# Convolution and attention in two layers: turn and sums in the score banks, the reciprocals in eight pieces, and the weighing two tiles behind

## The reference, cut to what matters

```python
# x: (8, 512, 32, 32), so B = 8 images, C = 512 channels, N = 1024 positions; 8 heads of D = 64
# layer 0: linear attention without softmax, batch norm over (image, position)
K, Q, V = conv1x1(X, Wq, bq), conv1x1(X, Wk, bk), conv1x1(X, Wv, bv)   # (b, 8, 64, 1024)
M = einsum('bhmn,bhen->bhme', K, V)
Out = conv1x1(einsum('bhme,bhmn->bhen', M, Q), Wo, bo) + X
Out = (Out - mean) * rsqrt(var + 1e-5) * gamma + beta
# layer 1: group norm, softmax attention, projection, residual
xn = group_norm(Out, 32 groups)
q, k, v = split(w_qkv @ xn + b_qkv)                                    # 8 heads each
weight = softmax((q / 64**.25)^T (k / 64**.25))                        # 1024 x 1024 per head
hid = v weight^T
return Out + w_proj @ hid + b_proj
```

## Time and profile before

| | before |
|---|---|
| median of 3 runs | 2682.73 us (2681.97 to 2682.75) |
| the profiled execution | 2683.36 us, its span 2681.8 us |
| TensorE matmul busy | 2582.5 us, 96% of the span |
| VectorE, ScalarE, GpSimd busy | 1621.5, 964.6, 1164.3 us |
| DMA over the span | 79 GB/s |

### The profile page before, as it was taken

How to read it: one execution, slowest core, us unless ns; L and a number is a source line. 1 busy time by engine, 2 the same in 40 slices (tenths; PEclk the granted TensorE clock), 3 DMA queues, 4 the chain that set the end, 5 groups by cost and what they waited for, 6 DMA issues and landing times.

```text
span 2681.8 us, 38121 instructions
## 1 busy us (share of the span) xinstructions
PE 2582.5 (96%) x13876; PEld 1710.9 (64%) x13876; DVE 1621.5 (60%) x1756; ACT 964.6 (36%) x1154; POOL 1164.3 (43%) x590
## 2 busy tenths in 40 slices
PE   7999999997999999999999999999999999999998
PEld 6888888886655665565557555755665565557554
DVE  6555455545576737755764667467647746664665
ACT  3333223332343433433442443343433433432433
POOL 4230000000276546564573676375654645761762
PEclk9999999999999999999999999999999999999999
DMA  5330111113202230231205111401231141103001
GB/s 185 130 132 33 47 47 63 63 63 111 110 24 79 87 126 24 95 128 70 102 17 181 40 79 61 152 24 80 102 110 41 78 175 38 79 18 109 17 16 63
DMA packets 64195, 214.34 MB, mean 80 GB/s; under 512 B 9152, under 2 KB 9152, under 8 KB 63168
## 3 DMA queue, kind: packets, MB, share of 16 engines
q1 hardware_dynamic: 49504, 159.41, 16.5%
q0 software_dynamic: 14560, 52.96, 5.4%
HBM read 141.05 MB, written 71.30 MB: 79 GB/s over the span
## 4 chain that ended last, share of the span: by engine, by line
PE 72%; DVE 15%; issue 6%; POOL 4%; ACT 2%; DVEq 0%; ACTq 0%; POOLq 0%
PE psum L1135 16%; PE psum L1380 14%; PE psum L1363 11%; PE psum L1320 7%; PE psum L1154 6%; PE psum L1330 5%; DVE a_all L999 4%; POOL a_all L528 4%; PE psum L1178 4%; PE psum L1206 3%; DVE small L964 3%; DVE r_all L955 2%; DVE r_all L1032 2%; ACT r_all L632 1%; PE psum L1252 1%
## 5 line engine op out<-in xcount | busy, mean ns | idle before, releaser
L528 POOL TENSOR_TENSOR a_all<-a_all 128x1024 f32<-128x1024 f32 x410 | 989.9, 2414 | 715.5 <-ACT a_all L701 680.6
L964 DVE TENSOR_REDUCE small<-psum 128x2 f32<-128x1024 f32 x481 | 589.3, 1225 | 377.8 <-PE psum L1330 377.6
L701 ACT ACTIVATE a_all<-psum 128x1024 f32<-128x1024 f32 x512 | 496.4, 1021 | 496.7 <-PE psum L1363 491.7
L1363 PE MATMUL psum<-r_all 64*128 64x512 f32 x4096 | 517.6, 391 | 1.5 <-ACT a_all L701 1.4
L1380 PE MATMUL psum<-a_all 128*64 128x512 f32 x2048 | 495.7, 605 | 1.4 <-DVE a_all L999 1.4
L1135 PE MATMUL psum<-r_all 128*128 128x512 f32 x1920 | 452.3, 393 | 7.0 <-DVE r_all L1032 5.8
L1363 PEld LDWEIGHTS psum<-r_all 64*128 64x128 f32 x4096 | 385.2, 185 | 88.9 <-ACT a_all L701 11.0
L1135 PEld LDWEIGHTS psum<-r_all 128*128 128x128 f32 x1920 | 357.6, 188 | 101.8 <-DVE r_all L837 11.6
L1320 PE MATMUL psum<-r_all 128*128 128x512 f32 x1536 | 377.2, 402 | 30.6 <-issue 11.8
L1320 PEld LDWEIGHTS psum<-r_all 128*128 128x128 f32 x1536 | 290.5, 192 | 133.6 <-DVE r_all L955 32.7
L1380 PEld LDWEIGHTS psum<-a_all 128*64 128x64 f32 x2048 | 124.3, 136 | 230.4 <-issue 174.0
(11 more groups left out here) (130 smaller groups left out, 1866.0 us busy)
## 6 DMA issues: line engine op xcount, KB each, us to landing
r_all<-w_dram SPq DMA_DIRECT2D x48, 1024.0 KB, 4.9
xn_dram<-a_all POOLq DMA_DIRECT2D x56, 512.0 KB, 3.8
r_all<-xn_dram SPq DMA_DIRECT2D x7, 4096.0 KB, 15.3
a_all<-y_dram SPq DMA_DIRECT2D x9, 2048.0 KB, 7.8
a_all<-x SPq DMA_DIRECT2D x16, 1024.0 KB, 6.6
y_dram<-a_all SPq DMA_DIRECT2D x16, 1024.0 KB, 4.2
out<-a_all SPq DMA_DIRECT2D x32, 512.0 KB, 3.2
w_dram<-r_all POOLq DMA_DIRECT2D x16, 512.0 KB, 3.6
```

The lines of the kernel that those rows point to most:

```text
L528: pool.tensor_tensor(p_sum[:, :, cols], probs[:, 0, :, cols] if i == 1 else p_sum[:, :, cols], probs[:, i % SLOTS, :, cols], ALU.add).then ...
L701: act.activation(probs[:, i % SLOTS, :, cols], psum[half][:, :, :], ACT.Exp, scale=SCALE).then_inc(probs_ready, 1)
L964: dve.reduce_max(max2[:, :, tile, half], psum[3][:, :, :], AX_X).then_inc(work_free, 2)
L1363: last = pe.matmul(psum[half][:, h], k[rows_], q[rows_], start=(t == 0), stop=(t == 3))
```

## The change

1. **Turn and sums move.** The turn goes to `psum[0]`, the sums to `psum[1]`, the two score banks, which are idle between two pairs. ScalarE copies the sums to SBUF (`copy_sums`), and the score halves of the first key tile wait until the turn is read and the sums are copied. The second q/k tile no longer stands behind the turn in `psum[3]`. For p = 0 the turn now comes ahead of the first q/k tile.
2. **Reciprocals.** They read the copy in SBUF, in place, in eight pieces of 128 columns: two after each of the first three q/k parts, the last two behind max tiles 1 and 3.
3. **The fourth q/k tile** goes to a bank of `psum[2]`, and the first max tile is an ordinary one in `psum[3]`.
4. **VectorE's other parts move back**: `normalise` behind max tiles 5 and 7 (before: ahead of and behind the first max tile), `hid_lo` behind 9 and 11 (before: 1 and 2). ScalarE's `hid_hi` moves behind the exponentials of key tiles 3 and 4.
5. **The weighing lags two tiles** (`LAG = 2`): S0 M S1 M S2 M W0 M S3 M W1 ... S7 M W5 M W6 M W7.
6. **Loops**: TensorE, VectorE and ScalarE's loops over the images of layer 1 get `hint_back_edge=True`, a branch hint at the head.
7. **M in layer 0** multiplies 128 columns in place of 256: the same 52 matmuls per image.

In the diff `copy_sums` stands in ScalarE's block, `invert_sums` and the loop over the max tiles in VectorE's, the rest in TensorE's. The two small copies for the next image's norm (line 1093), which stood behind max tile 4 of the pair p = 1, stand before the first max tile of p = 0 now.

```diff
-            def qk_tile(slot, i, before=lambda j: None):
-                piece, cols, to = i // 2, slice(i % 2 * HALF, (i % 2 + 1) * HALF), next_tile()
+            def qk_tile(slot, i, before=lambda j: None, fourth=False):
+                piece, cols = i // 2, slice(i % 2 * HALF, (i % 2 + 1) * HALF)
+                to = psum[2][:, 0] if fourth else next_tile()
...
-                pe.transpose(next_tile()[:, 0:P], max_cols.rearrange("p h t -> p (h t)"), eye).then_inc(work_full, 1)
-                return work.upto()
+                pe.transpose(psum[0][:, 0, 0:P], max_cols.rearrange("p h t -> p (h t)"), eye).then_inc(turn_full, 1)
...
+            def copy_sums(pairs):
+
+                act.wait_ge(o_normed, ONE + pairs * NH)
+                act.wait_ge(sums_full, ONE + pairs + 1)
+                act.activation(recip, psum[1][:, :, :], ACT.Copy).then_inc(sums_copied, 1)
...
+            def invert_sums(pairs, first, n):
+
+                if first == 0:
+                    dve.wait_ge(sums_copied, ONE + pairs + 1)
+                for piece in range(first, first + n):
+                    part = recip[:, piece // CT, piece % CT * P:(piece % CT + 1) * P]
+                    dve.reciprocal(part, part).then_inc(sums_inverted, 1)
...
-                        for m in range(1, MAXES):
+                        for m in range(MAXES):
                             max_tile(m)
-                            if p and m <= NH:
-                                hid_lo(b, p - 1, m - 1)
+                            if m == 0:
+                                next_qk(QK - 1)
+                            if p:
+                                if m in (1, 3):
+                                    invert_sums(pairs - 1, 6 + m // 2, 1)
+                                if m in (5, 7):
+                                    normalise(pairs - 1, m // 7)
+                                if m in (9, 11):
+                                    hid_lo(b, p - 1, m // 11)
...
                     for i in range(NT):
                         scores(pairs, par, i)
                         next_max()
-                        if i:
-                            weigh(b, p, i - 1, more)
+                        if i >= LAG:
+                            weigh(b, p, i - LAG, more)
                             next_max()
-                    weigh(b, p, NT - 1, more)
+                    for i in range(NT - LAG, NT):
+                        weigh(b, p, i, more)
+                        if i < NT - 1:
+                            next_max()
...
-            with pe.Fori(0, B - 1) as b:
+            with nc.Fori(0, B - 1, engines=[pe.engine], hint_back_edge=True) as b:
...
-                            pe.matmul(bank(g)[:, 0:2 * P], ts[:, t, o, g * P:(g + 1) * P], w_q[:, w, o, window],
+                            pe.matmul(bank(g)[:, 0:P], ts[:, t, o, part], w_q[:, w, o, part],
```

More of the change, by code:

```diff
@@ L625, in norm_row, with qk_hi @@
                 act.activation(hi_slot[:, j % 2], raw[j], ACT.Copy).then_inc(xn_hi_done, 1)
-            def qk_hi(pair, par, i):
-                n, ps = work.next()
-                act.wait_ge(work_full, n)
+            def qk_hi(pair, par, i, fourth=None):
+                if fourth is not None:
+                    ps = psum[2][:, 0]
+                    act.wait_ge(fourth_full, fourth)
+                else:
+                    n, ps = work.next()
+                    act.wait_ge(work_full, n)
                 of_k, cols = i // 2, slice(i % 2 * HALF, (i % 2 + 1) * HALF)
@@ L665, in batch1 @@
                     for i in range(QK):
[L666 to L667 removed]
                         if more:
[L669 to L671 removed]
+                            qk_hi((p + 1) % PAIRS, par, i, pairs + 1 if i == QK - 1 else None)
+                        if p and i == 0:
+                            copy_sums(pairs - 1)
                     for i in range(NT):
@@ L707, in batch1 @@
                     if more:
-                        for _ in range(MAXES - 1):
+                        for _ in range(MAXES):
                             work.next_pair()
@@ L723, in batch1 @@
                     norm_rows(range(1))
+                if not last:
+                    copy_sums(b * PAIRS + PAIRS - 1)
                 for h in range(NH):
@@ L947, in _, with qk_lo @@
             work = Tally()
-            def qk_lo(pair, par, i, count):
-                n, ps = work.next()
+            def qk_lo(pair, par, i, count, fourth=False):
+                ps = psum[2][:, 0] if fourth else work.next()[1]
                 of_k, cols = i // 2, slice(i % 2 * HALF, (i % 2 + 1) * HALF)
@@ L1097, in batch1 @@
                     else:
-                        normalise(pairs - 1, 1)
+                        invert_sums(pairs - 1, 0, PIECES)
+                        for h in range(NH):
+                            normalise(pairs - 1, h)
                         for i in range(1, NT):
@@ L1105, in batch1 @@
                     for h in range(NH):
[L1106 removed]
+                        invert_last(pairs, h)
                         normalise(pairs, h)
@@ L1111, in batch1 @@
                         v_tile(b + 1, i)
-                        if i in (1, 2):
-                            invert_sums(pairs, i - 1)
-                        if i in (3, 4):
-                            normalise(pairs, i - 3)
-                        if i in (5, 6):
-                            hid_lo(b, PAIRS - 1, i - 5)
+                        if 1 <= i <= 4:
+                            invert_sums(pairs, 2 * (i - 1), 2)
+                        if i == 5:
+                            for h in range(NH):
+                                normalise(pairs, h)
+                        if i in (6, 7):
+                            hid_lo(b, PAIRS - 1, i - 6)
                 for t, (o, half) in enumerate(proj_tiles(last)):
@@ L1332, in max_tile @@
                 last.then_inc(work_full, 2)
-            def max_first(par, pairs):
-                pe.wait_ge(sums_read, ONE + pairs * NH)
-                for h in range(2):
-                    rows_ = slice(h * D, (h + 1) * D)
-                    last = pe.matmul(psum[2][:, h], q_hl[rows_, par, HI, 0:P], k_hl[rows_, par, HI, 0:HALF], start=True, stop=True)
-                last.then_inc(max0_full, 1)
             def max_turn(pairs):
                 pe.wait_ge(max_ready, pairs + 1)
-                pe.transpose(next_tile()[:, 0:P], max_cols.rearrange("p h t -> p (h t)"), eye).then_inc(work_full, 1)
-                return work.upto()
+                pe.transpose(psum[0][:, 0, 0:P], max_cols.rearrange("p h t -> p (h t)"), eye).then_inc(turn_full, 1)
             def v_tile(i):
@@ L1356, in scores @@
                     pe.wait_ge(probs_ready, ONE + pairs * 2 * NT + (2 * (i - 1) + half + 1 if i else 0))
+                    if i == 0 and half == 0:
+                        pe.wait_ge(turn_read, pairs + 1)
+                    if i == 0 and half == 1:
+                        pe.wait_ge(sums_copied, ONE + pairs)
                     for t, (k, q) in enumerate(((k_hl[:, par, HI, keys], q_hl[:, par, HI, cols]),
@@ L1393, in sums @@
                     for h in range(2):
-                        last = pe.matmul(psum[2][h * D:(h + 1) * D, half], ones64, p_sum[:, h, half * HALF:(half + 1) * HALF],
+                        last = pe.matmul(psum[1][h * D:(h + 1) * D, half], ones64, p_sum[:, h, half * HALF:(half + 1) * HALF],
                                          start=True, stop=True)
                 last.then_inc(sums_full, 1)
+            LAG = 2
             pe.sem_inc(pv_done, ONE)
```

125 lines of the change are left out of this document (58 added, 67 removed).

## The result

| | before | after |
|---|---|---|
| median | 2682.74 us (2681.97 to 2684.0, 4 runs) | 2698.24 us (2696.07 to 2699.26, 4 runs) |
| the profiled execution | 2683.36 us, span 2681.8 | 2696.07 us, span 2694.6 |

The ratio is 1.0055 (95% interval 1.0042 to 1.0069): slower by 15.5 us, where +23.5 was forecast. As in the prediction, an insert is one of the four instructions (two `normalise`, two `hid_lo`) that VectorE does between max tiles, and a hold is the time by which GpSimd's next add comes later because of one.

The account below looks back on a forecast made before the run. TensorE's own list bounds the kernel, busy 49.1 of a pair's 50.16 us. Terms -11.5 - 20 + 62 - 3 - 4 = +23.5; 2683.4 + 23.5 - 0.6 = 2706 us, 8-in-10 range 2646 to 2757.

Parts of the forecast that it names:

- The inserts (+62): VectorE's `normalise` and `hid_lo` among max tiles wait for GpSimd's adds, locking rounds at 5.5 us: +62 us with first steps.
- The signs named for it: In pairs p > 0: rounds of 5.4 to 5.6 us, max tiles waiting 0.9 to 1.1, inserts of 2.3 to 2.6.
- Rival A: Inserts among max tiles stay as cheap as before, +5 us in the middle: 2649 us; chance 0.23.
- The hint (-20): At the head of the image loop, TensorE's idle 1.96 us and the half-clock stretch behind it go: -20 us.
- the waits of p = 0 (-11.5): The second q/k tile's 1.44 us wait in each p = 0 goes, as it has its own bank: -11.5 us.
- Rival C: At the image loop's head the hint does nothing, the gap being a fetch not reached in time: 2726 us; chance 0.08.
- M (-3): M in layer 0 at 128 columns keeps a pace of about 0.11 us, set by weight loads: -3 us.
- Rival B: M in layer 0 with 128 columns is slow, +48 in place of -3: 2757 us; chance 0.16.
- The reciprocals (0): VectorE's eight reciprocal pieces are hidden beside q/k tiles or fit the round's slack: 0 us, bounds 0 to +15.
- rival D: The reciprocals behind max tiles 1 and 3 also wait for adds, +15: 2721 us; chance 0.09.
- The last pair (-4): At the last pair's end, the final sums' 1.18 us wait goes and the 3.38 us wait for adds shrinks: -4 us.

Follow-up runs that it names:

- e2: The kernel before with only the two `normalise` behind max tiles 5 and 7, `hid_lo` behind 9 and 11, and `hid_hi` moved: 2726.87 us.
- e3: The changed kernel with the four inserts behind four max tiles in a row, 5, 6, 7 and 8: 2676.69 us.
- e4: The changed kernel with GpSimd's adds over 16 of each 512 columns, most of the sums left out: 2613.46 us.
- e5: The changed kernel with `normalise` behind max tiles 8 and 9, `hid_lo` at the pair's end, `hid_hi` behind key tiles 5 and 6: 2622.64 us.
- e9: e5 with the lag of the weighing at 1 instead of 2: 2619.01 us.
- e1: The kernel before with only the branch hint on the three loops over the images of layer 1: 2665.69 us.
- e10: The kernel before with only M over 128 columns in place of 256: 2681.41 us.
- e7: The changed kernel with each of GpSimd's adds made as two, one for each head: 2693.23 us.

## Why the prediction was right, and where it was off

*The inserts (+62), right in mechanism, too large by about a tenth.* All of it came as described: four waits in each pair p > 0, rounds locked to two adds and a hold, the reciprocals free of it; e2 makes the loss alone, e3, e4 and e5 set it to what the theory says. Two sizes were off. I took 0.6 us for the hold, which is how long the insert ends behind the add, and wrote that the add that follows is held up "for as long"; the numbers given for it, 2.78 against 2.45, say 0.33. So the round is 5.23 and not 5.5, 0.7 a pair too much. Against that the pair without waits is 49.2 [e4] and not 48.3 + 0.45, because a weighing with a max tile takes 2.30 at the end of the pair, where no score tile stands between (two of them, 0.2), and the first three steps lose nearly 0.6 and not 0.45. Net 2.5 a pair in place of 2.8. The signs named for it lie at the edge for the same reason: rounds of 5.2 to 5.4 against 5.4 to 5.6, and max tiles that wait 0.6 to 0.75 against 0.9 to 1.1; the inserts, at 2.3 to 2.4, are as named.

*Rival A (0.23) said that the same inserts are nearly free.* It was wrong for these places and right for others: an insert may wait up to 0.9 us without a max tile waiting [e9], and with the requests moved by two and three tiles and `hid_lo` at the end (e5) the time is 2623, 26 below A's 2649, since A kept the waits of the pair before. What I weighed as a doubt was a matter of phase.

*The hint (-20) and the waits of p = 0 (-11.5), right.* By the distances 21.1 for the hint [e1]. That leaves 11.5 for the seven waits at the boundaries, where 10.1 of the 11.5 were forecast; that it gives the forecast figure for eight is chance. The bank change was not run alone: e1 shows the wait of the second q/k tile without it, the changed kernel shows none. Rival C is out.

*M (-3), right*, and the sentences on it show how a rule is to be read. The Trainium skill, TensorE: Matmul & The Clock Gate, section "LDWEIGHTS (loading the stationary operand)", has a weight load at columns / 1.2, an estimate of 107 ns for 128 columns; the pace measured is 4 ns above it. The 56 ns taken from the same page's "Back-to-back issue gap" are for a matmul without its weight load, as that section says itself. For pairs of weight load and matmul it gives some 81 ns at 128 columns; here 111 were measured. The prediction and the expectation of e10 divided by 38 steps where there are 39, hence their 0.123 and 0.114 for what is 0.120 and 0.111; the term stays at -3 to -4. Rival B is out.

*The reciprocals (0), right*: 0.94 us each under the adds, 0.92 elsewhere, and rival D is out.

*The last pair (-4), mis-sized.* From the turn of the last pair to the end TensorE takes 69.9 us in place of 77.8. I had left out the wait of 1.36 for a reciprocal, which stands in the earlier trace rows, and the price of the idle stretch itself. Before, the eight matmuls of the sums take 3.6 us behind 3.38 us of idle time, at a granted clock of 0.50, 1.2 GHz:

```profile
2607.70:2611.30 3.60, 3.60 (x8) 0.83 (x8) 0.00 (x0) 0.00 (x0) 0.00 (x0) 0.50 0.00 0
```

The clock is still 0.58 in the next 2.7 us, and the two score tiles there take 5.46 us. After, the sums take 1.86 and two such tiles 4.7, at full clock. Here the wait that went took the slow stretch behind it along. With the 0.71 us that the sums still wait, these parts make 2.7 + 1.7 + 0.7 + 1.4 + 1.2 = 7.7 of the 7.9 us.

Open: up to the first score tile of layer 1 the traces of kernels with the same layer 0 differ by up to 2.3 us (727.5 to 729.8), so what M brings to that stretch can't be told within these, and the 1.6 us by which that term missed can't be read as its error.

## What to carry to other kernels

An instruction of one engine that must wait for a turn with another's long row of instructions has no fixed price. Here it cost from nothing to 1.0 us beside instructions of 2.4, by the phase of its request, and where the requests repeated in step with the pipeline the round locked to two adds and a hold, so that every one of them came at a bad moment. Before such instructions are moved, write down when the other engine's instructions end and when the request will come; place them where an end follows within the slack, or where nobody waits behind them. When the instruction that is waited for is cut in two, its total can grow, as in e7, so look at who waits for its last.

## What the runs showed of the hardware that was not expected

- A two-operand SBUF instruction of VectorE that gets in between two adds holds GpSimd back for 0.33 us only, though it takes 0.7 itself and ends 0.55 behind the add that it waited for. One that starts first holds the add for longer: 3.42 us in place of 2.4 in e9.
- A reciprocal of 128 x 128 from SBUF to SBUF takes 0.94 us beside the adds (27 of them) and 0.92 without; of the two small copies of 128 x 4 in the earlier trace rows the first ends 0.02 to 0.03 us behind the running add, in each of six images.
- GpSimd's add of 128 x 512 takes 1.37 us in the mean [e7], against 2.45 for 128 x 1024, holds included.
- The hint at the loop head removes some 1.96 us of idle time and 1.7 at half clock (4.38 against 2.72 us for twelve matmuls) in six rounds, and no cost of its own is seen there.
